# The causal mask of the own maxima: added by TensorE into the PSUM bank, or by VectorE in the operation that takes the maximum

## The reference

```python
att = jnp.einsum('bhqd,bhkd->bhqk', q, k) * scale
causal = jnp.tril(jnp.ones((T, T), bool))
att = jnp.where(causal[None, None], att, -jnp.inf)
y = jnp.einsum('bhqk,bhkd->bhqd', jax.nn.softmax(att, axis=-1), v)
...
attc = jnp.einsum('bhqd,bhkd->bhqk', qc, kc) * scale
y = y + jnp.einsum('bhqk,bhkd->bhqd', jax.nn.softmax(attc, axis=-1), vc)
```

## Time and profile before

| | us |
|---|---|
| median of 3 executions | 4895.98 |
| lowest and highest of them | 4895.41, 4904.88 |
| profiled execution, its own time | 4891.12 |
| span of the profiled execution | 4888.3 |
| PE busy | 4346.4 (89%) |
| DVE busy | 3532.4 (72%) |
| ACT busy | 2694.8 (55%) |
| POOL busy | 1646.7 (34%) |

### The profile page before, as it was taken

How to read it: one execution, slowest core, us unless ns; L and a number is a source line. 1 busy time by engine, 2 the same in 40 slices (tenths; PEclk the granted TensorE clock), 3 DMA queues, 4 the chain that set the end, 5 groups by cost and what they waited for, 6 DMA issues and landing times. The chain is left out here.

```text
span 4888.3 us, 75159 instructions
## 1 busy us (share of the span) xinstructions
PE 4346.4 (89%) x25317; PEld 1904.0 (39%) x25317; DVE 3532.4 (72%) x7733; ACT 2694.8 (55%) x5523; POOL 1646.7 (34%) x2163
## 2 busy tenths in 40 slices
PE   5999999999999999999999999999999995588882
PEld 2333333333343434333333333333333332477771
DVE  5788788787878787878787877887877783244443
ACT  1665656565655556565656565656565653344441
POOL 1122323232323232323232222323232314388883
PEclk7999999999999999999999999999999997799996
DMA  5453545444444444544444444444444443888888
GB/s 115 71 91 73 111 79 104 81 109 78 106 79 100 79 102 77 109 82 109 82 105 85 98 87 97 83 98 90 97 94 97 93 96 118 178 151 150 149 150 244
DMA packets 363500, 513.22 MB, mean 105 GB/s; under 512 B 64124, under 2 KB 227820, under 8 KB 363176
## 3 DMA queue, kind: packets, MB, share of 16 engines
q1 hardware_dynamic: 272592, 385.16, 37.8%
q0 software_dynamic: 87728, 115.39, 13.3%
q10 hardware_dynamic: 2856, 8.52, 0.5%
HBM read 288.49 MB, written 201.27 MB: 100 GB/s over the span
## 5 line engine op out<-in xcount | busy, mean ns | idle before, releaser
L662 ACT ACTIVATE prob<-scores 128x512 f32<-128x512 f32 (+3 forms) x4352 | 2150.3, 561 | 1331.3 <-PE scores L467 1297.4
L849 DVE TENSOR_REDUCE pmx<-ring 128x1 f32<-128x512 f32 (+1 forms) x3328 | 1998.5, 661 | 188.9 <-PE ring L545 175.6
L467 PE MATMUL scores<-stacks 98*128 98x512 bf16 (+3 forms) x4352 | 1272.3, 369 | 70.5 <-ACT prob L662 41.1
L489 PE MATMUL outs<-prob,vt 128*32 128x512 f32 x8704 | 1096.7, 576 | 12.7 <-POOL prob L1051 11.7
L545 PE MATMUL ring<-stacks 96*128 96x512 bf16 x3072 | 984.4, 389 | 90.1 <-DVE pmx L849 80.7
L467 PEld LDWEIGHTS scores<-stacks 98*128 98x128 bf16 (+1 forms) x4352 | 338.5, 99 | 1244.3 <-ACT prob L662 718.7
L849 DVE TENSOR_REDUCE mc<-ring 128x1 f32<-128x128 f32 (+3 forms) x1024 | 437.1, 480 | 147.1 <-PE ring L562 112.1
L1573 POOL DMA_INDIRECT scratch_sums<-e_yo,e_tok x320 | 495.9, 1550 | 118.8 <-issue 86.2
L1051 POOL TENSOR_SCALAR_AFFINE_SELECT prob<-prob 128x512 f32<-128x512 f32 x256 | 167.9, 656 | 1077.0 <-ACT prob L662 1075.2
L545 PEld LDWEIGHTS ring<-stacks 96*128 96x128 bf16 x3072 | 303.2, 99 | 511.4 <-DVE pmx L849 243.8
L1121 POOL TENSOR_TENSOR split<-rest,split 128x512 bf16<-128x512 f32 (+1 forms) x224 | 218.5, 975 | 824.4 <-DVE split L943 823.9
(11 more groups left out here) (165 smaller groups left out, 3752.7 us busy)
## 6 DMA issues: line engine op xcount, KB each, us to landing
stacks<-scratch_parts SPq DMA_DIRECT2D x768, 128.0 KB, 7.1
stacks<-scratch_parts SPq DMA_DIRECT2D x384, 136.1 KB, 10.1
scratch_parts<-split SPq DMA_DIRECT2D x64, 768.0 KB, 4.5
e_xin<-scratch_slots SPq DMA_DIRECT2D x160, 289.0 KB
scratch_parts<-split SPq DMA_DIRECT2D x32, 816.8 KB, 4.4
num<-oc POOLq DMA_DIRECT2D x256, 64.0 KB
den<-scratch_inverses POOLq DMA_DIRECT2D x63, 256.0 KB, 8.9
ct<-in_ctx_t_dram SPq DMA_DIRECT2D x16, 800.5 KB, 8.2
```

The lines of the kernel that those rows point to most:

```text
L467: eng.matmul(ps[0:m, k, q0:T], kst[g][0:KR + 2, j, k0:k0 + m], qst[g][0:KR + 2, j, qc + q0:qc + T], start=True, stop=True).then_inc(scored ...
L489: mm = eng.matmul(po[32 * j:32 * j + 32, q0:T], vt[ch][0:m, VW * vi + VE * hl:VW * vi + VE * hl + 32], prob[0:m, n % 2, j, q0:T], start=kt ...
L662: eng.activation(prob[0:m, n % 2, j, q0:T], ps[0:m, i % SB, q0:T], ACT.Exp, scale=SCALE).then_inc(exped.sem, 1)
L849: eng.tensor_reduce(dst, src, AX.X, ALU.max).then_inc(free_of(part, it), 1)
```

## The change

The second product of an own item goes, and with it identb and maskb. In its place there is one constant, mask_row, of 640 columns in bf16: 512 columns of 0 and then the 128 x 128 mask tile. DVE's operation on an own item becomes tensor_tensor_reduce: it adds the bank and a piece of mask_row (as many zero columns as the item needs and then the mask), writes the sums back over the bank, and puts their maximum out as accum_out. The tile zero becomes a view of the zero columns of mask_row. On POOL at the start one memset is larger and a copy and a memset go, so that CONSTS is 12. The plan with its costs, the ring, and all waits of the items stay.

```diff
-LOADS, CONSTS = 9 + 2 + 4 + 3 + 2, 14
+LOADS, CONSTS = 9 + 2 + 4 + 3 + 2, 12
...
-        identb = sb("identb", [128, 128], BF16)
-        maskb = sb("maskb", [128, 128], BF16)
+        mask_row = sb("mask_row", [128, T + 128], BF16)
+        zero = mask_row[:, 0:T].bitcast(F32)
...
-        zero = sb("zero", [128, C])
...
-                    eng.matmul(dst[:, 0:n], qst[g][0:KR, j, T + 128 * qt:T + n], kst[g][0:KR, j, 0:n], start=True, stop=False)
-                    eng.matmul(dst[:, 128 * qt:n], identb[:, :], maskb[:, :], start=False, stop=True).then_inc(ring.sem, 1)
+                    eng.matmul(dst[:, 0:n], qst[g][0:KR, j, T + 128 * qt:T + n], kst[g][0:KR, j, 0:n], start=True,
+                               stop=True).then_inc(ring.sem, 1)
...
-                    eng.tensor_reduce(dst, src, AX.X, ALU.max).then_inc(free_of(part, it), 1)
+                    if what == "own":
+                        eng.tensor_tensor_reduce(out=src, in0=src, in1=mask_row[:, T - 128 * it[3]:T + 128], scale=1.0, scalar=-3e38,
+                                                 op0=ALU.add, op1=ALU.max, accum_out=dst).then_inc(free_of(part, it), 1)
+                    else:
+                        eng.tensor_reduce(dst, src, AX.X, ALU.max).then_inc(free_of(part, it), 1)
...
-            eng.memset(maskb[:, :], 0.0).then_inc(consts.sem, 1)
+            eng.memset(mask_row[:, :], 0.0).then_inc(consts.sem, 1)
...
-            eng.affine_select(out=maskb[:, :], in_=maskb[:, :], compare_op=ALU.is_ge, fill=-1e30, base=0,
+            eng.affine_select(out=mask_row[:, T:T + 128], in_=mask_row[:, T:T + 128], compare_op=ALU.is_ge, fill=-1e30, base=0,
                               pattern=[[-1, 128]], channel_multiplier=1).then_inc(consts.sem, 1)
-            pool.wait_ge(consts, start, 3)
-            eng.tensor_copy(identb[:, :], ident[:, :]).then_inc(consts.sem, 1)
             eng.memset(tri[:, :], 1.0).then_inc(consts.sem, 1)
-            pool.wait_ge(consts, start, 6)
+            pool.wait_ge(consts, start, 5)
...
-            eng.memset(zero[:, :], 0.0).then_inc(consts.sem, 1)
```

## The result

| | before | changed |
|---|---|---|
| median of 20 executions each, us | 4898.61 | 4917.74 |
| lowest and highest, us | 4891.56, 4908.50 | 4900.56, 4929.09 |
| ratio of the changed kernel to the kernel before | | 1.0035, 95% interval [1.0025, 1.0046] |
| span of the profiled execution, us | 4888.3 | 4923.7 |
| mean granted clock of it | 0.961 | 0.949 |

The changed kernel is slower by 0.35% on this chip. Its time lies just inside the stated range, but on the other side of no change. The experiments ran on four other chips, always with the kernel before beside them; the whole change measured 1.0012 on one and 0.9997 on another, so its size depends on the chip. The granted clock is the share of TensorE's full clock (2.4 GHz) at which PE was let run. One execution of the twelve of run 5 took 5086.9 us at a clock of 0.824 and is left out of its numbers.

What follows compares the result with a forecast made beforehand. PE was taken to bound own stretches, DVE what follows g = 3. Gains of 0.5 + 0.9 + 0.9 - 0.4 = 1.9 us per batch element, times 16, gave 30 us: median 4866 us, own range 4846 to 4885, full range 4832 to 4920.

Steps and rivals of the forecast that it cites:

- What bounds the kernel: PE sets the pace in own stretches and mostly between them; DVE does behind g = 3, busy 48.80 of 52.90 us.
- the rival of hidden mask products: PE waits elsewhere as long, so removing mask products changes nothing and DVE's load shows: 4900 to 4915 us; chance 0.03.
- What goes from PE: In own stretches, 1024 mask products at 0.06 us leave PE: 61 us, 0.96 us a stretch, the most possible.
- a stretch of own items ends with the later of PE and DVE: Rule for summing each own stretch, with PE needing 0.96 us less and DVE 1.31 us more.
- What comes to DVE: On own items the new operation adds 5 + 77 = 82 ns each, 84 us in all, 1.31 us a stretch.
- The sign that PE's busy time would fall: Over the changed kernel, PE's busy time falls by less than 212 us, since the mask products' lengths overlapped.
- g = 2: Own stretch of g = 2: 0.5 us gained per batch element, as later banks take back about half of 0.96.
- g = 3: Own stretch of g = 3 and DVE's 53 us behind it: 0.4 us lost per batch element.
- g = 0 and 1: Own stretches of g = 0 and g = 1: 0.9 us gained in each per batch element.
- Small edits and blocking by POOL: At the start, ten microseconds cover the longer memset; on own items POOL does not block the new operation.
- DVE takes the gain back: In own stretches, an addition near 175 ns makes PE wait for banks: 4896 us, within 10 us; chance 0.13.
- the full gain: The maximum comes out free or DVE's slack covers it everywhere: 61 us less, 4835 us; chance 0.12.

Runs made afterwards that it cites:

- run 5: The changed kernel, new operation in all groups and no mask product, against the kernel before on another chip: 1.0012, mean clock 0.953.
- Run 2: Mask product left out and plain tensor_reduce kept, so the causal mask is missing from own maxima, against the kernel before: 0.9967, 4811.2 us.
- Run 1: The changed kernel with a 128-column PE product of zeros in the mask product's place, against the kernel before: 1.0036, 4846.0 us against 4827.4.
- runs 15 and 16: Kernel before with the new operation and a PE product with zeros for the mask product, in g = 3 alone (1.0011), in g = 0 and 1 (1.0015).
- run 10: The changed kernel with a 128-column product of zeros before each own product in g = 2 alone, against the kernel before: 0.9976, 4872.7 us.
- run 9: The changed kernel again, on the same chip as run 10, against the kernel before: 0.9997, 4883.4 us.

## Why the prediction was wrong, point by point

- **What bounds the kernel.** Right in the main: PE sets the pace of three of four parts. Run 2 shows that taking PE work away shortens the kernel, so the rival of hidden mask products fell, at least as a whole.
- **What goes from PE.** 1024 products at 0.06 us: right as work (in run 2, 32 us less busy time and 27 us more lost clock make 59). But "the most that the change can bring" was taken nearly whole in g = 0 and 1 (0.9 each), and run 2 got 16 us of 61 with no cost on DVE at all. The first step that failed is the rule "a stretch of own items ends with the later of PE and DVE". It compares sums over 11 us. With four banks the two engines take turns within a stretch: PE issues three or four own items in a half, then waits for banks, while DVE stands later. With PE's share shorter, its waits for DVE at own items grew by 12 us in run 2 with DVE unchanged; with the longer operation too they grew from 19 to 101 and by 23 us, and on the second chip from 18 to 120 and by 26. Slack of one engine in the sum is no cover in the order of the work.
- **What comes to DVE.** I took 5 + 77 = 82 ns an operation; it is about 50. The main part costs more than its neighbours (37 ns, not 5) and the accumulator read less (it runs beside the next main part). The size was on the safe side. Its effect was not: 84 us of DVE work were to cost 0.4 us per element in g = 3 and something in g = 2. Run 1 measured 17 us, and runs 15 and 16 found it in g = 0 and 1 too, where 2.95 and 2.65 us of slack were named as the cover.
- **The clock.** No term, no rival and no sign to look for: this is the second step that failed, a term that the sum put at nothing without a reason. Run 2 lost 27 us of the 61 to it, and the executions of run 5 lose 38 us of clock more than the kernel before on their chip. Waits and DVE's cost bring the gain near zero; where the result is a loss, the clock is low (0.949 on the first chip). The sign that PE's busy time would fall did not come there either: it rose by 13.5 us. I read the clock of 0.93 in the first of rows 1 and passed over it; the same loss was at work before the change. The Trainium skill (TensorE: Matmul & The Clock Gate, Part 1) says that the clock is throttled by default and that activity releases it. By that rule a change that takes short products out of PE's pauses could lower the clock, and it speaks against this change. The runs bear it out: run 10 against run 9.
- **g = 2.** Predicted 0.5 us gained per element; on the first chip the stretch and what follows grew by 0.85 us, on the second by 0.30. The term had the wrong sign; 2.04 and 0.95 us more of clock are lost there.
- **g = 3.** Predicted 0.4 us lost per element; 0.56 on the first chip, 0.57 on the second, from rows 11.42 + 53.26 against 11.48 + 53.76 of the table. This term was right in sign and near in size.
- **g = 0 and 1.** Predicted 0.9 us gained each. On the second chip they gained 0.43 and 0.16. On the first chip g = 0 lost 1.46, with 1.5 us of clock lost more behind it, and g = 1 gained 0.09.
- **Small edits and blocking by POOL.** Right: the new operation's longest is 737 ns, so POOL never held it, and the start is no later.
- **The rivals.** "DVE takes the gain back" gave 4896 for an addition near 175 ns. The outcome on the other chips (1.0012, 0.9997) looks like it, but its condition was not met: the addition was 50 ns, and the gain went to waits and to the clock. The prediction gives the full gain as 4835 in its rival and as 4832 in its range; nothing hangs on it.

## What to carry to other kernels

Before taking small work off PE, look at the clock column where the work stands: if it already falls there, the work may be what keeps it from falling more, and the test is a filler in that place alone. Compare two engines not by sums over a stretch but over what the buffers between them can hold. And try a change stage by stage: here it lost or was even as a whole and gained 0.6 to 0.7% in two of four groups. But measure the version that you mean to keep: the effects of the stages did not add.

## What the runs showed of the hardware that was not expected

- tensor_tensor_reduce with a maximum is a main part and an accumulator read of 140 ns, which overlaps the next main part; the pair takes 0.65 us from start to start at 512 columns where a reduce takes 0.60.
- Adding 256 products of zeros, each of 128 columns, in one stage made the kernel 10.7 us faster, at a mean clock of 0.958 instead of 0.952.
- Within 20 executions of the changed kernel on one chip the time follows the clock: 4900.6 us at 0.954, 4929.1 at 0.946. The spread of the kernel before is smaller (4891.6 to 4908.5).
- The kernel before took 4827 to 4899 us on five chips. Part of the difference stands in the stretch of g = 0 and behind it (66.85 us per element on the first, 63.52 on the second). The cause is open, and so is why the changed kernel loses 1.65 us of clock per element behind g = 0 on the first chip; run 10, on another chip, loses 1.0 there, and run 5 nothing.
